# Convolution taps moved to TensorE in 32x32 tiles, in chunks of 32 steps, inside a gated recurrence; state-space scan in slots of four batches

## The chip, the core and the metric

The kernel runs on one NeuronCore of a Trainium2 chip. It uses five engines: TensorE (PE in the rows, PEld for its weight loads), VectorE (DVE), ScalarE (ACT), GpSimd (POOL) and SyncE (SP), which here only issues DMAs. Each engine works through its own list of instructions in the order in which the program wrote them; between engines there are semaphores.

The metric is the device time of the core in microseconds. The kernel before took 2267.38, 2271.31 and 2275.32 us in three runs, 2271.31 in the median.

## The reference, cut to what matters

The input x is [32, 128, 128] (batch, step, feature), the condition [32, 128]. Eight layers follow each other. The first two are those that the change touches: a gated recurrence whose state has 128 features, and a state-space block on what it gives.

```python
def _L0_cond_ref(video, seq, W_z, U_z, C_z, b_z, W_r, U_r, C_r, b_r, W, U, C, b):
    vz = video @ C_z + b_z          # vr, vh alike
    xz = jnp.einsum('btd,de->bte', seq, W_z)     # xr, xh alike
    def step(h, xs):                # 128 steps, one after the other
        z = jax.nn.sigmoid(xzt + h @ U_z + vz)
        r = jax.nn.sigmoid(xrt + h @ U_r + vr)
        hh = jnp.tanh(xht + r * h @ U + vh)
        h_new = (1.0 - z) * h + z * hh

def _mamba2(x, W_in, conv_w, conv_b, dt_bias, A_log, D, init_states, norm_w, W_out):
    # D_INNER 256 = 8 heads x 32, N_STATE 64, CONV_DIM 384, D_CONV 16
    zxbcdt = x @ W_in               # z 256, xBC 384, dt 8
    dt = jax.nn.softplus(zxbcdt[..., -NHEADS:] + dt_bias)
    xBC = silu(causal depthwise convolution of xBC, 16 taps, + conv_b)
    xs, Bm, Cm = xBC[..., :256] (8 heads x 32), xBC[..., 256:320], xBC[..., 320:384]
    dA = jnp.exp(dt * A)            # A = -exp(A_log)
    def step(h, inp):               # h0 = init_states
        h = h * dA_t[:, :, None, None] + einsum('bh,bhp,bn->bhpn', dt_t, x_t, B_t)
        y_t = jnp.einsum('bhpn,bn->bhp', h, C_t)
    y = ys + D[None, None, :, None] * xs
    y = y * jax.nn.silu(z)
    y = y * jax.lax.rsqrt(jnp.mean(y * y, axis=-1, keepdims=True) + 1e-05) * norm_w
    return y @ W_out

def _L0_attn_ref(x, ...):
    y = _mamba2(x, ...)
    t = y / jnp.sqrt(1.0 + y * y)
    return t @ W_nl + b_nl + x
```

Then come a local attention with 16 heads (cond2 in the code), a mixture of experts, an LSTM, an attention with relative positions, a second LSTM and a second mixture of experts. The code of these stages is not changed, but for where the first of them (cprep) puts two transposed weights.

## The kernel before

Everything is kept with features on the 128 partitions. X [128, 32 batches, 128 steps] is the residual, G the output of the running layer. TensorE writes into eight banks of [128, 512] float32, which all carry the name B in the rows; mm (L85), act (L103), stt (L107) and ts (L112) are one-line helpers, so nearly all rows carry their lines, and a group is told by its tiles. The tiles work, catt and spare are large areas in which the stages lay their own buffers.

**Order.** There is no scheduler. For each engine and stage a generator issues instructions and yields; weave (L64) goes round the generators and takes one piece (a turn) of each. The lists of the engines thus come from the number of yields in each generator, written by hand; weave takes a lane out when it has ended.

**Recurrence** (gru_pe L407, gru_act L463, gru_dve L482, gru_pool L509), 22 to 250 us. A step is: the recurrent products of r and z with the tile gzh (mmh, L95: four column strips of 32 for each, since 32 batches are the columns), tanh on ScalarE into gth, VectorE's grh and gq, the product of the candidate with grh, tanh into ghh, VectorE's new gzh. Part of the next step's gate sum is put into the banks ahead with gq. The input products of the block of eight steps ahead (gru_inputs_pe L394, tile X) stand between the gate product and the candidate's, one piece a step, and gru_warm_pe (L448, tile identb) fills TensorE's idle time with a product of 384 columns behind each step and three more every fourth step, whose results are not used. Semaphores make POOL write each state to G.

**State space.** The 32 batches are worked on in eight units of four. Per unit the convolution (conv_pe L668, conv_act L695, conv_dve L736) takes three parts of 128 channels: a projection of G with win, an eviction by ScalarE into a padded buffer XP, taps 0 to 5 on TensorE as products with diagonal matrices (NT = 6, tile tap, 128x512 each), an eviction with the bias cb, and taps 6 to 15 on VectorE, one stt over [128, 512] each with the column cw; then tanh on ScalarE and one product for the SiLU on VectorE. The last part holds B and C in its two halves of 64 partitions.

The scan is done in matrix form, batch by batch, by two lanes (wk 0 and 1; mamba_pe L787, mamba_act L892, mamba_dve L978), which take the units in turn. One batch n of a lane goes: decay (eight scaled copies of the triangle tri, into E, catt in the rows), sums with the matrix low (two products of 512 columns), exponentials, cross (C times B, 64 rows deep, and the transposes of x), cbm and the product E times cbm (L1012), the state product with h0T, thirty-two 32x32 products of the triangle (with E and xdt), the product D x through the diagonal dg, the gate, and y on VectorE (L1020 to L1024). After four batches come norm, W_out, the long reciprocal (L1040), W_nl and two additions to X, the second on POOL (L1054). A unit of four batches has some 26 turns in each lane's list. mdt_pe, mdt_act, mdt_dve (L614 to L640) compute dt and the decays for all batches first.

**Around them.** mprep_load (L554) issues the loads of this stage's small weights on SP's queue; mprep_pe, mprep_act and mprep_dve prepare them inside the recurrence, h0T near its end. cprep, the preparation of the next stage, follows in lane 0's list, and mamba_first_end (L1104) is what it waits for.

## Time and profile before

| | before |
|---|---|
| runs | 2267.38, 2271.31, 2275.32 us |
| profiled execution: its own time / span | 2269.55 / 2267.7 us |
| mean granted TensorE clock | 0.951 |
| PE busy | 2011.8 us (89%), 25711 instructions |
| VectorE busy | 1698.1 us (75%), 3792 |
| ScalarE busy | 1008.1 us (44%), 2835 |
| GpSimd busy | 459.9 us (20%), 794 |

The profiled execution is one of its own. Its time lies 1.8 us under the median of the runs; its span goes from the first to the last instruction. The profile gives the shares of busy time over the whole span, so they mix stages with different limits. A row in order of time joins consecutive instructions of the same kind, and its second number then reaches from the first's start to the last's end.

By landmarks: the recurrence's last gzh starts at 250.0 us, the first decay at 278.9, the convolution's last taps end near 629, the last addition to X starts at 697.1, and the next stage begins at about 700.

### The profile page before, as it was taken

Reading aid. Unit: us, or ns where it says so; the run is one execution under the profiler, and the core shown is the slowest. Engines: PE = TensorE matmul, PEld = TensorE weight load, DVE = VectorE, ACT = ScalarE, POOL = GpSimd, SP = SyncE. Lnnn points to the kernel's source line nnn. Section 1 sums busy time; section 2 is a strip of 40 time slices with the busy share of each in tenths; the row PEclk is TensorE's granted clock in tenths of the full one; section 3 lists DMA queues with packets and bytes.
Section 4 is the critical chain, followed back from the end, with each engine's and each line's share of the span. In section 5 each row is a group of like instructions: output and inputs, shape, how many; then the busy total and the mean of one; then the engine's idle time right before and its main releaser. Section 6 shows DMA issues by size and latency. Waiting matters only on the chain.

```text
span 2267.7 us, 62486 instructions
## 1 busy us (share of the span) xinstructions
PE 2011.8 (89%) x25711; PEld 1278.0 (56%) x25787; DVE 1698.1 (75%) x3792; ACT 1008.1 (44%) x2835; POOL 459.9 (20%) x794
## 2 busy tenths in 40 slices
PE   7888888998886898898799999985999789999998
PEld 5555534444453444343576677763666556677776
DVE  3443489999965888777888888844999668888887
ACT  2333245666553221221555555542544445555555
POOL 2211000000000434336012222243432111121200
PEclk8999699999978999999999999996999999999999
DMA  2000000000010000000311111106553211111111
GB/s 61 3 4 4 2 1 1 1 1 1 1 38 15 0 1 1 1 1 1 112 48 44 44 44 44 39 4 130 107 108 73 65 40 44 39 44 44 44 57 38
DMA packets 76038, 76.61 MB, mean 34 GB/s; under 512 B 15756, under 2 KB 57060, under 8 KB 74180
## 3 DMA queue, kind: packets, MB, share of 16 engines
q1 hardware_dynamic: 71848, 70.11, 12.3%
q8 instruction: 203, 3.33, 0.6%
q10 hardware_dynamic: 3904, 2.49, 0.4%
q14 instruction: 83, 0.68, 0.1%
HBM read 60.09 MB, written 11.82 MB: 32 GB/s over the span
## 4 chain that ended last, share of the span: by engine, by line
PE 47%; DVE 30%; ACT 9%; issue 8%; DMA 1%; POOL 1%; ACTq 1%; SPq 1%; another core or an unknown queue 1%; DVEq 0%; POOLq 0%
PE B L85 46%; DVE work L107 6%; DVE work L2117 4%; DVE hr L2081 3%; DVE work L2125 3%; ACT work L103 2%; ACT hr L103 2%; ACT ltc L103 2%; DVE work L1496 1%; ACT catt L103 1%; DVE gzh L107 1%; ACT ghh L103 1%; DVE work L1040 1%; ACTq L2404 1%; DVE grh L107 1%
## 5 line engine op out<-in xcount | busy, mean ns | idle before, releaser
L85 PE MATMUL B<-gr,wres 128*128 128x512 f32 x1248 | 354.5, 412 | 16.4 <-DVE work L2125 10.1
L103 ACT ACTIVATE work<-B 128x512 f32<-128x512 f32 (+7 forms) x468 | 240.1, 529 | 145.4 <-PE B L85 90.2
L2167 POOL COPY G<-lh 128x32 f32<-128x32 f32 x256 | 148.2, 579 | 680.0 <-DVE lh L107 680.0
L85 PE MATMUL B<-work 128*128 128x128 bf16 (+3 forms) x1408 | 260.3, 312 | 28.0 <-ACT work L103 7.0
L85 PEld LDWEIGHTS B<-gr,wres 128*128 128x128 f32 x1248 | 215.1, 189 | 83.7 <-DVE work L2125 27.4
L103 ACT ACTIVATE hr<-work 128x512 fp32r<-128x512 f32 x272 | 173.0, 636 | 147.0 <-DVE work L2125 77.5
L85 PEld LDWEIGHTS B<-work 128*128 128x128 bf16 (+2 forms) x1408 | 141.4, 127 | 139.1 <-issue 79.9
L2081 DVE TENSOR_TENSOR hr<-work,hr 128x512 fp32r<-128x512 f32 x272 | 186.5, 686 | 8.1 <-ACT hr L103 6.6
L2117 DVE TENSOR_TENSOR work<-work 128x512 f32<-128x512 f32 x256 | 178.9, 699 | 16.1 <-ACT work L103 8.9
L107 DVE SCALAR_TENSOR_TENSOR work<-work,cw 128x512 f32<-128x512 f32 x240 | 179.2, 747 | 5.9
L85 PE MATMUL B<-hr,wres 128*128 128x512 f32 x624 | 178.0, 394 | 1.0 <-DVE hr L2081 1.0
L103 ACT ACTIVATE lth<-B 128x96 f32<-128x96 f32 (+1 forms) x512 | 86.8, 222 | 187.2 <-PE B L85 187.1
L85 PEld LDWEIGHTS B<-lh,lw 128*32 128x32 f32 x8128 | 88.8, 112 | 112.5 <-issue 58.6
L85 PE MATMUL B<-lh,lw 128*32 128x32 f32 x8128 | 117.0, 199 | 24.5 <-DVE lh L107 23.2
L107 DVE SCALAR_TENSOR_TENSOR work<-B,ckc,work 128x512 f32<-128x512 f32 x160 | 116.7, 742 | 27.1 <-ACT work L103 17.7
L103 ACT ACTIVATE catt<-catt 128x512 f32<-128x512 f32 (+3 forms) x141 | 81.8, 594 | 119.6 <-DVE catt L2417 89.4
L85 PEld LDWEIGHTS B<-hr,wres 128*128 128x128 f32 x624 | 117.2, 188 | 28.2 <-DVE hr L2081 1.9
L1496 DVE TENSOR_TENSOR work<-B,work 128x512 f32<-128x512 f32 x160 | 106.7, 681 | 32.2 <-remote 31.6
L107 DVE SCALAR_TENSOR_TENSOR lh<-lth,ltc 128x32 f32<-128x32 f32 x256 | 49.4, 193 | 106.6 <-ACT ltc L103 106.6
L1533 POOL TENSOR_TENSOR work<-work 128x512 f32<-128x512 f32 x64 | 82.2, 1284 | 209.7 <-DVE work L1496 115.5
L85 PE MATMUL B<-gr,hr 128*128 128x512 f32 x384 | 114.1, 434 | 10.0 <-DVE gr L1435 7.0
L85 PE MATMUL B<-X,lw 128*128 128x128 f32 x512 | 122.0, 323 | 0.0
(262 smaller groups left out, 3777.8 us busy)
## 6 DMA issues: line engine op xcount, KB each, us to landing
work<-wdr SPq DMA_DIRECT2D x128, 256.0 KB, 3.1
scr<-catt SPq DMA_DIRECT2D x144, 64.0 KB, 2.8
work<-scr SPq DMA_DIRECT2D x16, 384.0 KB
work<-scr SPq DMA_DIRECT2D x16, 192.0 KB
catt<-in_L_ffn_ew SPq DMA_DIRECT2D x24, 128.0 KB, 2.2
work<-scr SPq DMA_DIRECT2D x16, 128.0 KB
out<-work SPq DMA_DIRECT2D x32, 64.0 KB, 2.2
work<-in_x ACTq DMA_DIRECT2D x2, 512.0 KB, 5.3
```

The source lines that it names most:

```text
L85: return e.matmul(out, lhsT, rhs, start=start, stop=stop, skip_group_check=True)
L103: return e.activation(out, in_, func, bias=bias, scale=scale)
L107: return e.scalar_tensor_tensor(out=out, in0=a, scalar=s, in1=b, op0=op0, op1=op1)
L1040: e.reciprocal(m["tm"][:], m["tm"][:]).then_inc(*inc(me, "tr", i))
L1496: e.tensor_tensor(four(pr[n % 6]), four(B[:]), KP[:, c, :, j:j + 128], ALU.mult).then_inc(*inc(dve, "v", i, c, j))
L1533: e.tensor_tensor(av, u0, u1, ALU.add).then_inc(*inc(f"cd{wk}.pool", i, c))
L2081: e.tensor_tensor(hr[1][:], self.hh[j % 4], hr[0][:].bitcast(F32), ALU.subtract).then_inc(*self.inc("m.dve", "h", li, j))
L2117: e.tensor_tensor(src, self.sg[i], self.Wb[n % 4], ALU.mult).then_inc(*inc("m.dve", "pu", li, k))
L2125: h = stt(e, self.hh[m], U, 0.5, src, ALU.mult, ALU.mult) if li else e.tensor_tensor(self.hh[m], U, src, ALU.mult)
L2167: e.tensor_copy(self.G[:, :, t], self.lh[:, t % 4, :]).then_inc(*inc("l.pool", "h", li, t))
L2404: e.dma_start(self.aQ[u % 4][48 + q:49 + q, :, :], self.anT[16 * q:16 * q + 16, :]).then_inc(*self.dma("at.max", u))
```

## The change

The taps of the convolution leave VectorE altogether. The 384 channels are cut into twelve blocks of 32, and each of the sixteen taps is one call of conv_taps_pe: sixteen products on 32x32 tiles of the array. Tile (i, j) takes rows 32i to 32i+31 (channels) and columns 32j to 32j+31, and its moving operand is 8 batches x 32 steps, so block i of a part goes to bank 4+i and strip j holds the batches 8j to 8j+7. The stationary operand is a diagonal of 32, from the table tap [128, 48, 32] that POOL fills in steps 27 to 29 of the recurrence from id32 and cw.

The convolution goes by chunks of 32 steps instead of by units of batches: 4 chunks x 3 parts = 12 pieces (n), each with 16 tap calls, 4 projections of 8 batches (conv_input_pe, a 256-column product into bank 3 and an eviction by ScalarE) and 4 evictions with bias (in the last four pieces two of them by VectorE). Once the steps of a chunk are known, its convolution can run, so conv_pe and conv_act are called twice in each step of the recurrence from step 32 on, once between the gate and the candidate's product and once behind the step's input products; what is left (conv_rest_pe, conv_rest_act) runs after the recurrence and before both lanes. Up to step 31 warm-up products stand there, fewer than before.

To free banks for it, the recurrence keeps its sums in banks 0 to 2 (gru_place), and the input products of the block ahead move from between the two products to behind the step (gru_ahead_pe, five steps of eight). The conv's output cv is laid out [slot of 4 batches, block, step]: a slot o holds the batches o, o+8, o+16 and o+24, one in each 32 partitions.

The scan takes those slots. The transposes of x are done for half a slot at once (turn, bank 6+wk) and turned on VectorE into xdt and xD (with D in a row drow instead of through the diagonal dg, added in y as one more operation); B and C lie in 32 rows each, so cross and the state product become two products of 32 rows. SiLU (tanh and one product) goes into the lanes, four batches wide. Lane 1 starts 14 turns behind lane 0; a slot has 26 turns, and MAMBA_DT_TURNS and MAMBA_UNIT_TURNS go. The initial state h0T is turned for all four strips (mprep_pe, from step 4 on instead of near the end), the bias cb comes in 48 pieces of 32 rows, D in one load of a row.

```diff
-NT = 6
+CONV_STEP = 32
+CHUNK = 32
-MAMBA_DT_TURNS = 6
-MAMBA_UNIT_TURNS = ((8, 1, 1, 1), (22, 1, 1, 1))
+MAMBA_LAG = 14
@@ tensor (scalar alike; vector weaves mdt_dve with conv_dve first)
         weave(self.gru_pe(e), self.mprep_pe(e))
-        weave((self.mdt_pe(e), 2), chain(self.mamba_pe(e, 0), self.cprep_pe(e)), self.mamba_pe(e, 1), self.conv_pe(e))
+        self.conv_rest_pe(e)
+        weave(chain(self.mamba_pe(e, 0), self.cprep_pe(e)), self.mamba_pe(e, 1))
@@ gru_pe, each step
-            if t % 8 == 0 and t + 8 < T:
-                ahead = chain(self.gru_inputs_pe(e, g + 1, 0), self.gru_inputs_pe(e, g + 1, 1))
-            next(ahead, None)
-            if t % 4 == 0:
-                self.gru_warm_pe(e, t, 3)
+            elif t >= CONV_STEP:
+                next(conv, None)
+            elif t % 2:
+                self.gru_warm_pe(e, t, 1)
             e.wait_ge(*at("gru.rh", t))
...
-            self.gru_warm_pe(e, t, 1)
+            self.gru_ahead_pe(e, t)
+            if t >= CONV_STEP:
+                next(conv, None)
+            else:
+                self.gru_warm_pe(e, t, 1)
@@ gru_ahead_pe
+        g, x = t // 8 + 1, t % 8
+        if g == T // 8 or x > 4:
+            return
...
+        if x < 4:
+            self.gru_inputs_pe(e, g, odd, x // 2)
+        else:
+            self.gru_inputs_z_pe(e, g)
@@ mprep_load
+        for k in range(12):
             for j in range(4):
-                pairs.append((self.dcol[32 * j:32 * j + 32, c:c + 1],
-                              bc(I["L0_attn_D"][4 * c + j:4 * c + j + 1], 0, 32)))
-        for c in range(3):
-            pairs.append((self.cb[:, c:c + 1], col(I["L0_attn_conv_b"][c * 128:c * 128 + 128])))
+                pairs.append((self.cb[32 * j:32 * j + 32, k:k + 1], col(I["L0_attn_conv_b"][32 * k:32 * k + 32])))
@@ mprep_pe
-        for _ in range(T - 6):
+        for _ in range(4):
             yield
         e.wait_ge(*self.at("ld.mamba"))
@@ conv_rest_pe (was mdt_pe)
         for b in range(NB):
             last = mm(e, P[:, b, :], self.G[:, b, :], self.win[:, 640:648], True, True)
         last.then_inc(*self.inc("mdt.pe", "x"))
-        for _ in range(12):
-            yield
+        for _ in self.conv_rest:
+            pass
@@ conv_taps_pe
+        for j in range(4):
+            for i in range(4):
+                r = slice(32 * i, 32 * i + 32)
+                last = mm(e, self.bank[4 + i][32 * j:32 * j + 32, 0:256], self.tap[r, 16 * c + k, :],
+                          self.XP[c][r, 8 * j:8 * j + 8, k:k + CHUNK], k == 0, k == 15)
@@ conv_pe
+        for j in range(4):
+            self.conv_input_pe(e, 0, j)
+            yield
+            yield
+        for n in range(12):
+            k = 0
+            for x in range(20):
+                if x in (12, 14, 16, 18):
+                    if n == 11:
+                        continue
+                    self.conv_input_pe(e, n + 1, (x - 12) // 2)
+                else:
+                    self.conv_taps_pe(e, n, k)
+                    k += 1
+                yield
+            for _ in range(4):
+                yield
@@ conv_out_dve
+        return (2, 3) if n >= 8 else ()
@@ conv_dve: the taps 6 to 15 go
-                for k in range(NT, 16):
...
-                    stt(e, acc, X[:, :, 1 + k:129 + k], self.cw[:, c, k:k + 1], acc, ALU.mult, ALU.add).then_inc(
@@ mamba_pe: cross and the state product
-            mm(e, B2[:, 256:384], cv[0:64, 2, t_], C0[0:64, t_], True, True)
-            for c in range(2):
-                last = e.transpose(B2[:, c * 128:c * 128 + 128], cv[:, c, t_], self.ident[:])
+            for x in range(2):
+                last = mm(e, B2[:, 256:384], cv[r, 8 + x, :], cv[r, 10 + x, :], x == 0, x == 1)
...
-                for c in range(2):
-                    mm(e, B0[:, c * 128:c * 128 + 128], cv[:, c, t_], self.dg[:, c, :], c == 0, False)
-                mm(e, B0[:, 256:512], C0[0:64, t_], self.h0T[:], False, False)
+                for x in range(2):
+                    mm(e, B0[:, 256:512], cv[r, 10 + x, :], self.h0T[r, x, :], x == 0, False)
@@ mamba_dve, per half slot (turned)
+            e.tensor_tensor(m["xdt"][:, hs], B3, bc(self.dth[:, o:NB:8, hs].rearrange("p j h -> p h j"), 3, 32), ALU.mult)
+            e.tensor_tensor(m["xD"][:, hs].rearrange("p h j q -> p h (j q)"), B3.rearrange("p h j q -> p h (j q)"),
+                            bc(self.drow[:, hs], 2, 128), ALU.mult).then_inc(*inc(me, "xd", i, h))
```

What this makes of the lists is seen at three places. First TensorE's list at step 40 of the recurrence; gzh feeds the gate product, grh the candidate's, gq the part put in ahead, X,gw are the input products, identb the warm-up. Before:

```order
L85 MATMUL B<-gzh,gw 32x32 x8
L85 MATMUL B<-X,gw 128x32x4
L85 MATMUL B<-grh,gw 32x32 x4
L85 MATMUL B<-gq,gn 32x32 x8
L85 MATMUL B<-identb 128x384
L85 MATMUL B<-gzh,gw 32x32 x8
```

And now, where "work 32x256 x16" is one call of taps:

```order
L85 MATMUL B<-gzh,gw 32x32 x8
L85 MATMUL B<-work 32x256 x16
L85 MATMUL B<-grh,gw 32x32 x4
L85 MATMUL B<-gq,gn 32x32 x8
L85 MATMUL B<-X,gw 128x32x4
L85 MATMUL B<-work 32x256 x16
L85 MATMUL B<-gzh,gw 32x32 x8
```

The input product has moved from between the gate and the candidate's product to behind the step, and a call of taps stands in both places.

Second, TensorE's list in steps 4 and 5, with what now stands there:

```order
L85 MATMUL B<-gzh,gw 32x32 x8
L85 MATMUL B<-grh,gw 32x32 x4
L85 MATMUL B<-gq,gn 32x32 x8
L85 MATMUL B<-gV,ident 128x256
L85 MATMUL B<-X,gw 128x32x4x2
L85 MATMUL B<-identb 128x384
L85 MATMUL B<-ident,h 32x128 x4
L85 MATMUL B<-gzh,gw 32x32 x8
```

The products "ident,h" turn the initial state; they wait for all loads of mprep_load, and the next step's gate product stands behind them. Before they stood near the step 122.

Third, TensorE's list in the scan, at the end of a unit of one lane beside a batch of the other. Before:

```order
L85 MATMUL B<-work,wout 128x512 x2
L85 MATMUL B<-work 128x512 x3
L85 MATMUL B<-catt,low 128x512 x2
L85 MATMUL B<-work 128x512 x3
L85 MATMUL B<-dg,work 128x128 x2
L85 MATMUL B<-h0T,work 128x256
L85 MATMUL B<-work,catt 32x32 x32
L85 MATMUL B<-G,win 128x512
L85 MATMUL B<-win,G 128x256
L85 MATMUL B<-work 128x128
L817 MATMUL B<-ident,work 128x128 x2
L85 MATMUL B<-work,wnl 128x512
```

And now:

```order
L85 MATMUL B<-work,wout 128x512 x2
L85 MATMUL B<-catt,low 128x512 x2
L85 MATMUL B<-h0T,work 128x256 x2
L85 MATMUL B<-spare,catt 32x32 x32
L85 MATMUL B<-win,G 128x256
L85 MATMUL B<-work 128x128 x2
L85 MATMUL B<-work,wnl 128x512
```

The taps (work 128x512), the projection (G,win) and the diagonal (dg) are gone from between the lane's products; the transposes (L817) have become half a slot at once and stand at the end of a unit.

On VectorE, in the same stretch, before:

```order
L1024 TENSOR_TENSOR work<-work,catt 128x256
L107 SCALAR_TENSOR_TENSOR work<-work,cw 128x512 x3
L1004 TENSOR_TENSOR work<-B,triq 128x128
L1007 TENSOR_TENSOR work<-B,catt 128x256
L1012 TENSOR_TENSOR catt<-catt,work 128x1024
```

And now, at the same operations of a lane (L1102 is cbm, L1105 the product of 1024, L1117 to L1121 are y):

```order
L107 SCALAR_TENSOR_TENSOR catt<-catt,B 128x256
L1102 TENSOR_TENSOR spare<-B,triq 128x128
L1105 TENSOR_TENSOR catt<-catt,spare 128x1024
L107 SCALAR_TENSOR_TENSOR X<-B,bnl,X 128x4x128
L107 SCALAR_TENSOR_TENSOR work<-catt,work 128x512
```

The taps are gone, the products of xdt (L1007) too; a SiLU product of 512 elements stands in some turns.

## Rows read from the trace of the kernel before

**Rows 1.** Busy by stretches: us; PE, PEld, DVE, ACT, POOL (count); clock; DMA; GB/s
```profile
22.00:250.00 228.00, 197.58 (x5532) 122.09 (x5531) 94.73 (x534) 75.57 (x442) 48.50 (x149) 0.95 0.02 4
250.00:262.00 12.00, 11.20 (x53) 11.01 (x52) 0.38 (x2) 0.02 (x1) 0.55 (x4) 0.50 0.00 1
350.00:600.00 250.00, 226.59 (x2044) 116.34 (x2043) 232.59 (x379) 153.33 (x370) 8.86 (x5) 0.99 0.00 1
625.00:650.00 25.00, 20.32 (x178) 10.96 (x179) 18.39 (x38) 15.87 (x38) 1.27 (x1) 0.73 0.01 2
```

**Rows 2.** Groups by shape, 350 to 600 us: busy us, mean ns | idle before
```profile
L107 DVE SCALAR_TENSOR_TENSOR work<-work,cw 128x512 f32<-128x512 f32 x160 | 119.3, 746 | 3.7
L1012 DVE TENSOR_TENSOR catt<-catt,work 128x1024 f32<-128x1024 f32 x22 | 26.7, 1214 | 0.0
L107 DVE SCALAR_TENSOR_TENSOR work<-work 64x512 f32<-64x512 f32 x10 | 11.7, 1166 | 0.3
L85 PE MATMUL B<-work 128*128 128x512 f32 x189 | 85.9, 595 | 2.3 <-ACT work L103 2.3
L85 PE MATMUL B<-G,win 128*128 128x512 f32 x32 | 17.2, 620 | 0.0
L103 ACT ACTIVATE work<-B,cb 128x512 f32<-128x512 f32 x16 | 10.9, 682 | 2.8 <-PE B L85 2.8
L103 ACT ACTIVATE work<-B 128x512 f32<-128x512 f32 x31 | 18.3, 596 | 20.8 <-PE B L875 17.1 <-PE B L85 3.7
```

**Rows 3.** Order of time, one recurrence step: start us, us, engine, instruction
```profile
101.36 0.33 PE L85 MATMUL B<-gzh,gw 128*32 128x32 f32 x16
101.62 0.49 PE L85 MATMUL B<-X,gw 128*128 128x128 f32 x2
102.24 0.27 PE L85 MATMUL B<-grh,gw 128*32 128x32 f32 x8
102.34 0.33 PE L85 MATMUL B<-gq,gn 128*32 128x32 f32 x16
102.61 0.34 PE L85 MATMUL B<-identb 128*128 128x384 bf16 x1
103.06 0.33 PE L85 MATMUL B<-gzh,gw 128*32 128x32 f32 x16
```

**Rows 4.** Tile gzh: ns min/median/max, first and last start us
```profile
L107 DVE SCALAR_TENSOR_TENSOR gzh<-gth,ghh x128: 179/193/771, 27.6 to 250.0; 128x32 f32<-128x32 f32 x128
L85 PE MATMUL B<-gzh,gw x2048: 196/196/263, 22.7 to 248.7; 128*32 128x32 f32 x187
```

**Rows 5.** Order of time, TensorE, on the full array and in three column strips
```profile
569.91 5.33 PE L85 MATMUL B<-work 128*128 128x512 f32 x12
807.45 1.06 PE L85 MATMUL B<-work,selh 128*32 128x512 f32 x6
```

**Rows 6.** SyncE's queue in order of time; DMA issues, us to landing last
```profile
17.69 1.37 SPq L572 DMA_DIRECT2D cb<-in_L_attn_conv_b  x3
cb<-in_L_attn_conv_b SPq DMA_DIRECT2D x3, 0.5 KB, 2.0
```

**Rows 7.** Order of time, TensorE, 250 to 266 us
```profile
250.99 13.82 PE L85 MATMUL B<-win,G 128*128 128x8 f32 x64 [0.80 <-POOL G L112]
```

**Rows 8.** Order of time, state space, from 630 us to its end
```profile
633.04 2.43 ACT L103 ACTIVATE catt<-tri,catt 128x128 f32<-128x128 f32 x8
636.75 3.65 PE L85 MATMUL B<-catt,low 128*128 128x512 f32 x4
646.04 2.43 ACT L103 ACTIVATE catt<-tri,catt 128x128 f32<-128x128 f32 x8
648.52 1.98 PE L85 MATMUL B<-catt,low 128*128 128x512 f32 x4 [0.34 <-ACT catt L103]
655.45 2.44 ACT L103 ACTIVATE catt<-tri,catt 128x128 f32<-128x128 f32 x8
697.11 1.26 POOL L1054 TENSOR_TENSOR X<-X,G 128x512 f32<-128x512 f32 x1 [36.38 <-DVE X L107]
```

509 lines of the change are left out of this document (284 added, 225 removed).

## The prediction, made before the result was known

> **What bounds the kernel now.** On the page PE is the busiest engine, but its share is an average over stages, so the busy time by stretches comes first. In the recurrence (22 to 250 us) no engine is full of useful work: it is a chain of 128 steps. In the state space VectorE is busy 232.6 of 250 us and TensorE 226.6, ScalarE only 153.3 [rows 1]. The reader is to see that both leading engines are full there, and in the second view (groups by shape, 350 to 600 us) with what: on VectorE 160 taps of 746 ns, 119.3 us, and on TensorE 85.9 us of taps and 17.2 us of the convolution's input projection [rows 2]. Last the order of time in three places: a step of the recurrence, tiles side by side in the array, and the end of the state space, where no tap is left.
>
> A step: the gate product starts at 101.36, the candidate's at 102.24, the next gate product at 103.06: 1.70 us, paced by hops PE, ACT, DVE, PE [rows 3]. PE has two holes. The first runs from +0.26 (another tile shape enters 0.26 us after the sixteen gate records begin) to +0.88, the second from +1.25 to +1.70. The 127 intervals from 27.6 to 250.0 us [rows 4] are 1.75 us in the mean.
>
> **The change, part by part.** Sums are against the profiled execution, 2269.55 us (span 2267.7); the runs' median, 2271.31, is 1.8 higher.
>
> *1. Price of a tap call:* 16 matmuls on 32x32 tiles, 256 columns, a pair of records each (every f32 matmul shows as two). On the full array twelve records of 512 columns take 5.33 us, 0.44 each, so 0.22 for 256 columns. Three column strips take 1.06 us for their six records of 512 [rows 5]: strips run at once, a strip's two halves behind each other. If all sixteen tiles do, a call lasts 1.06 - 0.44 (256 columns) + 13 more tiles x 8 ns (sixteen gate records end within 0.33 us [rows 3] where one lasts 0.20 [rows 4]) = 0.72 us by the record. The next shape can start 0.06 us before such an end, as the warm-up does behind the sixteen records of 102.34 (102.61 against 102.34 + 0.33 [rows 3]): 0.66 net. Back to back I take 0.46. No row shows tiles that differ in their 32 rows, so 0.66 is one end; the others are the rivals B (1.30) and E (3.7). I take 0.66, since the row with tiles shows overlap.
>
> *2. A load ahead of step 4.* The convolution's bias comes in 48 pieces instead of 3, D in one instead of 8: 38 more issues of SP at 1.37/3 = 0.46 us, 18 us. Today the last is issued at 19.06 us and lands 2.0 us later [rows 6]; now at about 39. PE used to wait for these loads only near the end of the recurrence; now the turned copies of the initial state stand in step 4, some 7 us after 27.6, at 34.8. The whole chain stands behind them: 4 us, plus 1 for the clock, whose mean of 0.95 in this stage [rows 1] says that it falls at times. +5.
>
> *3. Recurrence, steps 32 to 127.* 192 holes take 126 tap calls and 30 input projections. First hole, 48 taps: 0.26 + 0.66 = 0.92 against 0.88, +0.04, 2 us. An input (0.49 us for two records of 128 columns [rows 3], + 0.22) costs about as much as it has slack. Second hole, 78 taps: 1.25 + 0.66 = 1.91 against 1.69, +0.22. But the next block's input products now stand there too, ahead of the tap, in five steps of eight: 0.49 us by the record, 0.43 net [rows 3], the fifth with twice the columns, +0.22. That gives 0.22 / 0.65 / 0.87 in 3 / 4 / 1 of 8 steps, 0.52 in the mean; 70 x 0.52 + 8 x 0.22 (no block ahead after step 119) = 38. Sum +40 us. ACT is busy 75.6 of 228 us in this stage [rows 1], so I take it that its evictions of 256 columns (under the 0.60 of 512 [rows 2]) fit its gaps. POOL's three products for the tap table stand in steps 27 to 29, covered by the two steps of slack that VectorE leaves it.
>
> *4. The rest of the convolution* cannot hide: both lanes start behind it. 32 small products take 13.8 us today [rows 7], mostly at the lower level (granted 0.50 [rows 1]), so some 7 at the upper one; I take 8. Then 66 tap calls x 0.46 = 30, 14 inputs x 0.72 = 10, and five stalls for evictions, one of 1.9 us (ACT alone) and four of 0.9: 5.5. Together 54 us: from 295 (250 + 40 + 5) to 349 us. VectorE's softplus chain lies beside it.
>
> *5. State space.* The floor of what stays, per unit (one batch; 22 in those 250 us, by the L1012 row): ACT 153.3 less the convolution's 30 (10.9 + 32 x 0.60) over 22 is 5.6, plus 0.5 for the tanh: 6.1 us. TensorE 226.6 - 103.1 over 22: 5.6. It loses the diagonal product and gets two 32-row matmuls in place of each 64-row one, not shown: from nothing to twice their time, and neither is on the way to more than the ACT figure. VectorE 232.6 less 119.3, 11.7 and some 7 (SiLU) [rows 2] over 22 is 4.3; plus some 1.2 for the SiLU and the two 128x512 products of a half slot: 5.5. Hence 32 x 6.1 = 195 us at least.
>
> But a lane is a chain: decay (2.43), sums (1.98), state and tile products, gate product, tanh, next decay. From 646.04 to 655.45, without taps and with the other lane in its norm, a unit takes 9.4 us; from 633.04 to 646.04, in part at the lower clock (the sums took 3.65) and with the last SiLU, 13.0 [rows 8]. A lane spends ten of a slot's 26 turns outside its units, and the lanes are 14 turns apart. So of a slot pair's eight units four run beside the other's norm, two at 9.4 and two at 10.5 (the 13.0 at the upper level, without SiLU): 40 us. The other four share ten turns, bound by ACT at 5.6 each: 22 us. With 4 us for spells at the lower level 66 us, 2.54 a turn; now it is 8 x 250/22 = 91 us. Lane 1 ends after 124 turns: 28 alone at 9.4/4 = 2.35, 66 us, and 96 x 2.54 = 244. Sum 310, from 349 to 659 us.
>
> The last addition to X starts at 697.1 us now [rows 8]. 659 against 697: -38 us. Later stages keep their instructions. 2269.6 - 38 = 2232.
>
> **Rivals.**
> A, the forecast: 2232.
> B, slower: *row tiles of one column strip wait for each other*. A tile's second half, standing ahead of the next row tile in its strip, holds it back: five spans of 0.22 instead of two, +0.64 a call; it decides above 0.86 us a call. Every hole is already overfull: 126 x 0.64 = 81, and 66 x 0.64 = 42 behind: 2355. For it: strips visibly keep their own order; against it: nothing but that strips are independent.
> C, *the scan goes at the lower clock level*. The dense taps leave it; today, where they end, the granted clock is 0.73 [rows 1]. With the tail's units at 13.0 a turn takes 3.05: 96 x 3.05 + 28 x 2.7 = 368, +58, less 3: 2287, slower too. Against it: at 648.52 the sums are back at 1.98 [rows 8].
> D, *the lanes pack to the engines' floor*: 52 us per pair, 96 x 2.0 + 28 x 2.1 = 251, -59: 2173. For it: VectorE is 93% busy today.
> E, *strict order*: half, half, next tile, one after the other: 17 x 0.22 = 3.7 us a call, 192 x 3.0 = 580 more, some 2800. Against it: in strict order the three strips would need four times 0.44, not 1.06 in all [rows 5].
> E is what the Trainium skill states ("TensorE: Matmul & The Clock Gate", Part 3: matmuls start and end in program order); the rows for column strips disagree with it. The same part measures 10.6 times for sixteen tiles, which speaks for A; no row here shows row tiles.
>
> **How the numbers follow.** A 0.43, D 0.18, B 0.24, C 0.14, E 0.01. 0.3% (6.8 us) is what a measurement can tell from no change. A's own spread (+-30 us) puts 0.37 of it under the bound, 0.04 inside, 0.02 over; D is all faster; C has 0.02 faster and 0.02 the same. Faster 0.57, same 0.06, slower 0.37. The range goes from a little under D to B: 2168 to 2357; A's own is 2202 to 2262.
>
> **What would show it.** Right: recurrence steps of 1.75 to 2.4 us after step 32; tap calls of 0.7 us with sixteen tiles overlapping; a stall of 4 us at step 4; the last step near 295, the first decay near 349; a slot pair in 66 us. B: calls over 1.2 us, steps over 2.6. C: a granted clock under 0.8 from 350 to 660 us, sums of 3.6 us. D: ACT over 90% busy. Wrong altogether if later stages move by over 5 us.

## The result, and the profile after

The changed kernel takes 2379.99 us in the median of four runs (2373.37 to 2391.22), the kernel before 2271.23 us in four: ratio 1.0484, 95% interval 1.0436 to 1.0532. It is slower by some 109 us, where 2232 was forecast and the range ended at 2357. The profiled execution took 2384.33 us, its span 2382.1.

| stretch, us | before | forecast | after | after less forecast |
|---|---|---|---|---|
| first gzh to step 32 | 60.0 | 65 | 82.2 | +17 |
| steps 32 to 127 | 162.5 | 202 | 248.3 | +46 |
| last step to first decay | 28.8 | 54 | 90.8 | +37 |
| first decay to last addition to X | 418.2 | 310 | 353.7 | +44 |
| from there to the end | 1570.6 | 1571 | 1581.0 | +10 |

A stretch is read from the starts of gzh's products on VectorE, of the first decay and of POOL's last addition. The last row is no effect of the change: in the runs below, whose instructions there are the same, it lies anywhere from 1569 to 1582. The other four are where the forecast failed. They vary too from trace to trace where the lists are the same: steps 32 to 127 take 242.6 to 251.9 us in nine traces with the lists of the changed kernel, the scan 349.4 to 355.8 in ten; the first stretch repeats within 1 us. A smaller difference between two traces shows nothing.

The busy time by stretches of the changed kernel, with the columns of [rows 1] and to be held against them:

```profile
22.00:107.00 85.00, 68.07 (x1436) 41.49 (x1435) 25.79 (x135) 19.70 (x111) 20.99 (x57) 0.58 0.04 3
107.00:357.00 250.00, 219.79 (x8018) 119.76 (x8017) 65.79 (x382) 75.59 (x380) 33.16 (x101) 0.93 0.02 4
357.00:447.00 90.00, 74.83 (x2207) 49.30 (x2206) 15.23 (x37) 10.95 (x29) 2.16 (x4) 0.85 0.01 3
447.00:801.00 354.00, 274.98 (x2760) 150.92 (x2760) 203.33 (x369) 210.39 (x517) 10.97 (x9) 0.76 0.02 7
```

The reader is to see two things. In the scan no engine is full any more (TensorE 78%, ScalarE 59%, VectorE 57%), so the floors of the engines, from which half of the forecast's part 5 (state space) is worked out, bound nothing. And the granted clock is 0.58 in the early recurrence and 0.76 in the scan.

The first four lines of what TensorE waited for, 22 to 447 us (us in total, times, longest):

```profile
PE B L85 <- issue: 23.2, 36, 1.2
PE B L85 <- DVE grh L107: 18.8, 32, 1.4
PE B L85 <- DVE work L112: 7.8, 3, 3.0
PE B L85 <- DMA cb<-in_L_attn_conv_b: 4.6, 1, 4.6
```

The fourth line is the load of part 2 of the forecast: 4.6 us for 4 forecast. The second is the first hole of a step, where no input product stands any more: 18 of its 32 waits, 11.2 us, lie before step 32, where the kernel before has two of 1.1 us together. The first line is one that the forecast does not have, and it is the largest: "issue" is a wait for nothing that the profile shows. In order of time, TensorE with its records in two steps of the recurrence (start us, us, engine):

```profile
...
187.27 0.65 PE L85 MATMUL B<-work 32*32 32x256 f32 x11 [0.95 <-issue]
187.84 0.27 PE L85 MATMUL B<-grh,gw 128*32 128x32 f32 x8
187.93 0.31 PE L85 MATMUL B<-gq,gn 128*32 128x32 f32 x16
188.17 0.77 PE L85 MATMUL B<-work 32*32 32x256 f32 x32
188.87 0.33 PE L85 MATMUL B<-gzh,gw 128*32 128x32 f32 x16
189.13 0.76 PE L85 MATMUL B<-work 32*32 32x256 f32 x32
189.82 0.27 PE L85 MATMUL B<-grh,gw 128*32 128x32 f32 x8
189.90 0.23 PE L85 MATMUL B<-gq,gn 128*32 128x32 f32 x5
191.00 0.32 PE L85 MATMUL B<-gq,gn 128*32 128x32 f32 x11 [0.86 <-issue]
```

A call of taps (32 records) takes 0.76 us, near the forecast's 0.72, but TensorE stops in the middle of one call (21 of its records stand before the first row), and again in the middle of sixteen gq records, whose operand has been there since the first five. The first time it idles 0.95 us, the second 0.86. Behind the recurrence, where calls follow each other:

```profile
434.73 2.75 PE L85 MATMUL B<-work 32*32 32x256 f32 x128
438.20 2.76 PE L85 MATMUL B<-work 32*32 32x256 f32 x128 [0.72 <-issue]
441.67 2.76 PE L85 MATMUL B<-work 32*32 32x256 f32 x128 [0.71 <-issue]
```

After every 128 records it stands still for 0.71 us. 128 records with their 128 weight loads are 256 entries, and the transfers of the instruction queue are 16 KB each. In 40 us of the recurrence, 180 to 220 us, there are eight of them before and eleven after:

```profile
q8 instruction: 8, 0.13, 1.4%
```

```profile
q8 instruction: 11, 0.18, 2.2%
```

So 256 entries would be one such transfer (64 bytes each, worked out and not shown by a row). The changed kernel makes one per 3.6 us where the one before made one per 5, and back to back it gets one per 3.47 us. The times of the transfers fit: from 428 to 447 us there are four, which start at 432.38, 435.89, 439.33 and 442.81 us, and TensorE goes on 2.3 us behind each, at 434.73, 438.20, 441.67 and 445.14. I take it that this is the pace at which TensorE is supplied here; the experiments test it.

### The profile page after: what moved, and what is told of

It is laid out like the page before. It is cut to its first block, busy times and chain, and to the rows that moved or that the text cites. A ratio compares the mean times of both kernels' runs of the same rounds, so it can differ in the third digit from the quotient of the medians.

```text
span 2382.1 us, 73929 instructions
## 1 busy us (share of the span) xinstructions
PE 2078.9 (87%) x31509; PEld 1311.7 (55%) x31509; DVE 1544.3 (65%) x3565; ACT 1010.8 (42%) x2862; POOL 467.0 (20%) x806
## 4 chain that ended last, share of the span: by engine, by line
PE 56%; DVE 22%; ACT 9%; issue 8%; SPq 2%; DMA 1%; ACTq 1%; POOL 1%; DVEq 0%; POOLq 0%
PE B L85 54%; DVE work L2220 4%; DVE work L107 3%; DVE hr L2184 3%; DVE work L2228 3%; ACT catt L103 2%; ACT hr L103 2%; ACT ltc L103 2%; SPq L630 1%; ACT work L103 1%; ACTq L2507 1%; DVE work L1599 1%; DVE lth L107 1%; DVE lpq L107 1%; DVE gr L2034 1%
## 5 line engine op out<-in xcount | busy, mean ns | idle before, releaser
L85 PE MATMUL B<-work 32*32 32x256 f32 (+2 forms) x7328 | 294.0, 385 | 27.1 <-issue 11.2
L103 ACT ACTIVATE work<-B 128x512 f32<-128x512 f32 (+6 forms) x480 | 236.8, 509 | 174.0 <-PE B L85 131.7
L85 PEld LDWEIGHTS B<-work 32*32 32x32 f32 (+2 forms) x7328 | 162.6, 108 | 124.4 <-issue 75.8
L85 PE MATMUL B<-lh,lw 128*32 128x32 f32 x8128 | 116.9, 199 | 24.5 <-DVE lh L107 23.2
L85 PE MATMUL B<-catt,low 128*128 128x512 f32 x128 | 96.2, 898 | 38.8 <-ACT catt L103 33.4
L107 DVE SCALAR_TENSOR_TENSOR grh<-gth,gh 128x32 f32<-128x32 f32 x128 | 28.0, 218 | 143.4 <-ACT gth L103 143.4
```

What stands on the lines that cost most here:

```text
L85: return e.matmul(out, lhsT, rhs, start=start, stop=stop, skip_group_check=True)
L103: return e.activation(out, in_, func, bias=bias, scale=scale)
L107: return e.scalar_tensor_tensor(out=out, in0=a, scalar=s, in1=b, op0=op0, op1=op1)
```

## Experiments

Positions are those of the profiled execution; the totals are medians of four runs, the ratios are to the kernel before, timed beside it.

### a1, a2: the wait for the load, and the warm-up

a1, of the changed kernel (its other half delays ScalarE's copy likewise):

```diff
 def mprep_pe
-        for _ in range(4):
+        for _ in range(20):
             yield
```

> The turned copies of the initial state move from steps 4 to 7 of the recurrence to steps 20 to 23, behind the landing of the bias pieces; nothing else changes. Theory 'the wait lets the clock fall': in the changed kernel TensorE waits 4.6 us in step 4, the granted clock falls to 0.50 at 38 us and comes back only at 120 us, and steps 5 to 35 cost some 2.5 us instead of 1.9. Without the wait the clock stays up: the recurrence ends some 20 us earlier (336 instead of 356.6), total near 2360. Rival 'only the wait': 5 us, total near 2375, and the clock falls all the same, because the warm-up has become thin.

a2 adds the old amount of warm-up below step 32:

```diff
-            elif t % 2:
-                self.gru_warm_pe(e, t, 1)
+            elif t % 4 == 0:
+                self.gru_warm_pe(e, t, 3)
```

> As a1, and up to step 31 the warm-up of the kernel before (three products more every fourth step, in place of one in every odd step). If the clock falls for the thin warm-up and not for the wait, a1 gains 5 us and this one 20; if the wait was the cause, both end alike within 3 us; if the clock falls in both, the low level belongs to something else that the change put there (the input products behind the step).

Measured: a1 2371.58 us (ratio 1.0451, 1.0434 to 1.0469), a2 2370.03 us (1.0449, 1.0417 to 1.0482); step 32 starts at 100.2 and 103.7 us instead of 108.4. The stop of 4.6 us is gone, and the stretch up to step 32 is 9.0 us shorter in a1 (73.2 for 82.2), 4.7 in a2. So the theory that the wait alone lets the clock fall is wrong (20 us expected); "only the wait" (5 us, and the clock falls all the same) is nearer, and the old warm-up does not bring the clock back: from 38 to 90 us it is 0.64 and 0.60 (0.50 in the changed kernel, 0.90 before). The trace of a2 shows what the forecast had not priced. First the kernel before at the lower level, then a2 at the same level:

```profile
47.53 0.44 PE L85 MATMUL B<-gzh,gw 128*32 128x32 f32 x16
47.90 0.80 PE L85 MATMUL B<-X,gw 128*128 128x128 f32 x2
48.63 0.34 PE L85 MATMUL B<-grh,gw 128*32 128x32 f32 x8
48.76 0.42 PE L85 MATMUL B<-gq,gn 128*32 128x32 f32 x16
49.11 0.50 PE L85 MATMUL B<-identb 128*128 128x384 bf16 x1
49.54 0.44 PE L85 MATMUL B<-gzh,gw 128*32 128x32 f32 x16
```

```profile
46.05 0.44 PE L85 MATMUL B<-gzh,gw 128*32 128x32 f32 x16
47.00 0.33 PE L85 MATMUL B<-grh,gw 128*32 128x32 f32 x8 [0.51 <-DVE grh L107]
47.18 0.44 PE L85 MATMUL B<-gq,gn 128*32 128x32 f32 x16
47.55 0.80 PE L85 MATMUL B<-X,gw 128*128 128x128 f32 x2
48.14 0.52 PE L85 MATMUL B<-identb 128*128 128x384 bf16 x1
48.59 0.44 PE L85 MATMUL B<-gzh,gw 128*32 128x32 f32 x16
```

Before, the input product X fills the first hole and a step at the lower level takes 2.01 us without a gap. Now the hole stands empty (0.51 us idle) and X stands in the step's own path: 2.54 us. It costs once in the step, and TensorE idles in addition; whether that keeps its level low is what c2 asks.

### b1, c2: the input products back in the first hole, and filling

b1 is a1 with the input products of r and the candidate between the gate and the candidate's product again, two steps later (z's share a bank with what ScalarE reads there, so they stay); c2 is b1 with more warm-up up to step 31: one or three products in the first hole and two behind each step. The edit of b1:

```diff
+                if t >= 2 and (t - 2) % 8 < 4:
+                    self.gru_ahead_pe(e, t - 2)
...
-            self.gru_ahead_pe(e, t)
+            if t % 8 == 4:
+                self.gru_ahead_pe(e, t)
```

> As a1, and the input products of r and the candidate for the block ahead go back between the gate product and the candidate's, two steps later than now (steps 2 to 5 of a block; z's stays behind step 4 because of its bank). Theory 'the empty hole and the input products in the path': up to step 31 a step loses the 0.8 us of input products at the lower level and TensorE no longer idles 0.5 us in the first hole, so the clock comes back by 60 us as in the kernel before: the recurrence ends 15 to 20 us earlier than in a1 (348), with step 32 starting at 88 to 92 instead of 100. Rival 'something else holds the clock down' (taps, chip): step 32 within 3 us of 100. From step 32 on both agree on no gain: one hole loses what the other gets.

> As b1, with warm-up products in the first hole and two behind every step up to step 31. If the low clock in steps 5 to 31 comes from thin filling together with the moved input products, step 32 now starts at 85 to 90 us as in the kernel before (96.6 in b1, 100.2 in a1, 108.4 in the changed kernel), and the total is 5 to 10 us under b1's; if it starts at 96 again, the filling is not it.

Measured: b1 2365.11 us (1.0413, 1.0383 to 1.0442), step 32 at 96.6, the recurrence ends at 344.4; c2 2355.22 us (1.0365, 1.0334 to 1.0397), step 32 at 90.3, its end at 332.3. In c2 the granted clock is 1.00 from 38 to 90 us. b1 alone gave less than half of what was expected, 3.6 us where it was 8 to 12 at step 32; with the filling, step 32 is back within 3 us of the kernel before (87.6). The first miss is thereby taken apart. Of the 22.2 us by which the stretch from the first gzh to step 32 grew (60.0 to 82.2), taking away the wait for the load gives back 9.0 (a1: 73.2), the input products back in the hole 3.2 (b1: 70.0) and the filling 6.1 (c2: 63.9); 3.9 stay open. So the load is the largest part, twice the 4.6 us of its stop. The shares are for this order of edits.

### a3: all taps behind the recurrence

```diff
-CONV_STEP = 32
+CONV_STEP = 128
```

> All 192 calls of taps and all 48 projections behind the recurrence, warm-ups in their place. Theory 'the holes are worth it': the recurrence ends near 260 to 270 us (86 us of the steps from 32 on and part of the low clock go), then 192 calls of 0.87 us (0.69 and a quarter of a 0.7 us stop), 48 projections of 0.7 and twelve waits of 2.7 us: 230 us, first decay near 505 us instead of 447, total near 2435. Rival 'the holes are as dear as the place behind': first decay within 15 us of 447 and a total within 15 us of 2380, because each call in a hole lengthens its step by almost what it costs behind.

Measured: 2482.93 us (1.0945, 1.0919 to 1.0970), the recurrence ends at 318.1 us, the first decay starts at 548.7: 101 us later than in the changed kernel, nearly twice the 58 that were expected. The recurrence then runs at the lower level for 244 of its 291 us (102 of 330 in the changed kernel, 20 of 222 before) and ends at 318 instead of 260 to 270. The part behind takes 230.6 us, as worked out (230). The holes are worth using: the rival, no difference, is wrong by 100 us.

### a4, d1, b2, c4: what a call of taps is bound by

a4 puts four products of 96 columns on the full array in place of the sixteen, d1 (on top of c2) eight on 64x64 tiles, b2 keeps table and input in bfloat16, c4 swaps the two loops.

```diff
 a4, conv_taps_pe
+        if 0 < k < 15:
+            for i in range(4):
+                mm(e, self.bank[4 + i][:, 0:96], self.ident[:], self.XP[c][:, 8 * i:8 * i + 8, k:k + 12], False, False)
+            return
 d1, conv_taps_pe
+                        mm(e, self.bank[4 + 2 * i + h][64 * j:64 * j + 64, 0:256], self.ident[r, 64 * i:64 * i + 64],
+                           self.XP[c][r, 8 * j:8 * j + 8, k:k + CHUNK], False, False)
 b2, lay_mamba
-        self.tap = ar(128, 48, 32)
-        self.XP = [ar(128, NB, CHUNK + 15) for _ in range(3)]
+        self.tap = ar(128, 48, 32, dt=BF16)
+        self.XP = [ar(128, NB, CHUNK + 15, dt=BF16) for _ in range(3)]
 c4, conv_taps_pe
-        for j in range(4):
-            for i in range(4):
+        for i in range(4):
+            for j in range(4):
```

> In place of the sixteen 32x32 products of calls 1 to 14 of every block of taps, four products on the full array of 96 columns each (the taps' values are left out, calls 0 and 15 stay): 8 records of some 85 ns, 0.68 us of array time as before, with a quarter of the instructions. Theory 'TensorE is starved of instructions': its stops that nothing releases (30 times, 19 us up to 360 us, and eight of 0.53 to 0.82 us behind) go, the recurrence ends 20 us earlier and the rest behind it is 10 us shorter: total near 2350. Rival 'the holes are too short for 0.7 us': the stops go elsewhere or cost nothing, total 2372 to 2385.

> The table of taps and the padded input are kept as bfloat16, so each of a call's sixteen products shows as one record instead of two: half the instructions of a call and a quarter of the columns' time (the taps are less exact by this). In the changed kernel calls that follow each other take 0.69 us and TensorE then stops 0.7 us after every 128 records. Theory 'a call is bound by the instructions': back to back a call takes half, 0.33 to 0.36 us, the stops that nothing releases halve (36 times to under 20), the recurrence ends near 315 and the first decay near 380; total near 2310. Rival 'bound by the columns' (16 tiles' 256 columns pass one after another per strip): 0.2 us a call or less. Rival 'the holes are not the cause': recurrence still over 345.

> The sixteen tiles of a call go in the other order: the column strip changes from product to product instead of the rows. In the changed kernel a call's 32 records take 0.71 to 0.76 us, 0.69 when calls follow each other. If a call is bound by the rate at which products start, nothing changes: a call in 0.69 to 0.76 us, total within 8 us of 2380. If tiles of one strip hold each other back, a call is shorter (0.5 us) and the total falls by over 15 us; if tiles of the same rows do, it gets longer.

> As c2, but calls 1 to 14 of every block of taps go on 64x64 tiles: eight products of 256 columns instead of sixteen (the taps' values are left out, since the identity stands in place of the table). Each tile still passes two products one after the other, 0.43 us by the columns' time, with half the instructions. Theory 'stops for instructions': back to back a call takes 0.45 us, hardly any stop in the recurrence is left, a step from 32 on costs 2.1 to 2.2 us instead of 2.55 (242 us for 95 steps in c2), so the recurrence ends near 295 instead of 332, and the part behind it takes 65 instead of 88: total near 2295. Rival 'hole too short, instructions do not matter': recurrence within 8 us of c2's.

Measured: a4 2440.26 us (1.0744, 1.0706 to 1.0782), b2 2342.5 us (1.0288, 1.0249 to 1.0327), c4 2382.53 us (1.0494, 1.0474 to 1.0513), d1 2360.13 us (1.0384, 1.0367 to 1.0400, against 1.0365 of c2).

a4's stops are gone up to its first decay (none is left), as the theory of the instructions has it, but its time got worse: the clock is at the lower level for 256 of 395 us of the recurrence, which its expectation did not have; why is not shown. So a4 does not price the stops, hence d1. c4: nothing changes, so neither strips nor rows hold a call back. b2, TensorE behind the recurrence:

```profile
388.21 1.90 PE L85 MATMUL B<-work 32*32 32x256 bf16 x117 [1.87 <-DVE work L112]
391.62 2.00 PE L85 MATMUL B<-work 32*32 32x256 bf16 x128 [1.51 <-issue]
395.36 0.43 PE L85 MATMUL B<-work 32*32 32x256 bf16 x11 [1.75 <-issue]
```

Up to its first decay b2 stops 8 times for "issue", 8.4 us, where the changed kernel stops 36 times, 23.2 us. Its recurrence is 27 us shorter (303.1) although 239 us of it are at the lower level. (b2's profiled execution, 2325.66 us, was the fastest of its four runs, 17 under their median.)

d1's own price was wrong: a call on 64x64 tiles takes 1.03 us, not 0.45 (from the start of the first line to that of the second), so that the recurrence ended at 337.4 and not near 295. That is within 8 us of c2's 332.3, the very bound of the rival "instructions do not matter"; the total alone cannot tell the two apart:

```profile
203.69 1.09 PE L85 MATMUL B<-work,ident 64*64 64x256 f32 x16
204.71 0.27 PE L85 MATMUL B<-grh,gw 128*32 128x32 f32 x8
```

The waits can. What TensorE waited for from step 32 to the end of the recurrence, c2 and then d1:

```profile
PE B L85 <- issue: 18.7, 27, 1.7
PE B L85 <- DVE gzh L107: 6.7, 18, 0.4
PE B L85 <- DVE grh L107: 4.4, 8, 0.6
```

```profile
PE B L85 <- DVE gzh L107: 6.4, 18, 0.4
PE B L85 <- DVE grh L107: 4.4, 8, 0.6
```

All stops are gone and the other waits are the same. d1's calls are 0.34 to 0.38 us longer (1.03 against 0.65 to 0.69 net, from a call's start to the next tile's), 14 of 16 of the 126: 37 to 42 us more; its steps 32 to 127 took 247.6 us where c2's took 242.0, 6 more. So the stops cost an estimated 31 to 36 us there, give or take the 5 us by which this stretch varies, and more than the 18.7 that show as idle. The difference lies in slow calls, as that of 1.40 us instead of 0.71 at 202.31 us in the changed kernel; that they are slow for the same reason is not shown by itself.

### b3, c1, d2, e2: level and table loads in the scan

b3 puts two unused products before the sums of three batches in four, c1 ten there and four before the state product; d2 replaces the norms' square roots by copies, e2 is c1 with d2.

```diff
 c1, mamba_pe
                 yield
+                if j:
+                    self.fill_pe(e, B3, 10)
                 if n < 15:
                     sums(n + 1)
                 yield
                 if j:
+                    self.fill_pe(e, B3, 4)
 d2, mamba_act (the same for m["tm"])
-            act(e, m["ss"][:], m["ss"][:], ACT.Sqrt).then_inc(*inc(me, "sr", i))
+            act(e, m["ss"][:], m["ss"][:], ACT.Copy).then_inc(*inc(me, "sr", i))
```

> In the scan two unused products of 384 columns stand before the sums of three batches in four, where TensorE waits for the decays. Theory 'the scan goes at the lower level': granted 0.76 over 354 us in the changed kernel (172 us at the lower level, the sums 1061 ns in the median instead of 592); with the holes filled the clock rises over 0.9 and the scan takes 325 us or less: total near 2350. Rival 'the chain of a lane is paced by ScalarE and VectorE': the clock rises but the scan stays within 8 us of 354. Third way: the products delay the other lane's sums by 0.7 us each, 24 times a lane, and the scan gets longer, 365 or more.

> Two such products in b3 were too few: 384 columns in bfloat16 are 0.16 us at the upper level, TensorE was still idle a fifth of the scan, the lower level went from 172 to 135 us and the scan from 353.7 to 352.1. Here, in the changed kernel, ten stand before the sums of three batches in four (where TensorE waits 2.2 us for the decays) and four before the state product. Theory 'the lower level stretches the lanes' chains' (sums 3.7 us instead of 2.0, once or twice a unit): lower level under 80 us, scan 325 us or less, total near 2350. Rival 'the lanes are held by ScalarE's order (table loads and the norm's square root between a batch's decay and its exponentials)': the scan stays within 8 us of 354 even at the upper level. If the products themselves delay the other lane: over 362.

> In the changed kernel, the square roots of the norms are replaced by copies (those values are left out), so ScalarE no longer loads a table before and behind each: up to 32 loads of 1.28 us in the scan. Theory 'ScalarE's order holds the lanes' (at 630.3 to 633.1 and 644.4 to 647.6 us one lane's loads stand between the other's sums and its exponentials): 16 pairs of loads, 41 us of ScalarE, of which more than half is on a lane's chain: scan 325 to 335 instead of 353.7, total near 2360. Rival 'something else, the loads lie beside waits': scan within 8 us of 354.

> c1 and d2 in one: the scan filled as in c1, and the norms' square roots replaced by copies (those values are left out), so no table loads. If the two waits hide each other, the scan gains far more than 5 + 3 us: 325 to 335 instead of 353.7. If they do not, it takes 344 to 347, the sum of the two, and the lanes are held by the order of the lists and the chain itself.

| kernel | total us | ratio, interval | at the lower level | scan us |
|---|---|---|---|---|
| changed | 2379.99 | 1.0484, 1.0436 to 1.0532 | 172 | 353.7 |
| b3 | 2373.46 | 1.0440, 1.0417 to 1.0463 | 135 | 352.1 |
| c1 | 2373.66 | 1.0456, 1.0434 to 1.0478 | 83 | 349.0 |
| d2 | 2381.02 | 1.0475, 1.0459 to 1.0490 | 172 | 350.9 |
| e2 | 2367.16 | 1.0418, 1.0397 to 1.0439 | 61 | 341.6 |

Ten traces whose scan lists are those of the changed kernel take 349.4 to 355.8 us, so b3, c1 (4.7 us) and d2 (2.8 us) by themselves show no clear gain; each time the rival ("within 8 us of 354") was right. Both together give 12.1 us, which is clear, in the scan as in the total. It is more than the sum of 7.5 that was expected if the two do not hide each other, and far from 325 to 335. How they can hide each other is seen in the changed kernel's scan:

```profile
640.50 0.60 ACT L103 ACTIVATE spare<-B 128x512 f32<-128x512 f32 x1 [2.50 <-PE B L85]
640.99 2.43 ACT L103 ACTIVATE catt<-tri,catt 128x128 f32<-128x128 f32 x8
643.47 3.78 PE L85 MATMUL B<-catt,low 128*128 128x512 f32 x4 [3.01 <-ACT catt L103]
644.35 1.28 ACT L103 ACT_TABLE_LOAD   x1
646.30 1.28 ACT L103 ACT_TABLE_LOAD   x1
647.59 1.08 ACT L103 ACTIVATE catt<-B 128x512 f32<-128x512 f32 x2
```

Lane 0's decays (640.99) stand behind a square of lane 1 for which ScalarE waits 2.50 us. Then come the sums, at the lower level until 647.2, and ScalarE's loads around lane 1's square root until 647.58, so that the exponentials (647.59) are late by either. In c1 the same place reads:

```profile
642.25 1.98 PE L85 MATMUL B<-catt,low 128*128 128x512 f32 x4 [1.39 <-ACT catt L103]
643.13 1.28 ACT L103 ACT_TABLE_LOAD   x1
645.07 1.28 ACT L103 ACT_TABLE_LOAD   x1
646.37 1.08 ACT L103 ACTIVATE catt<-B 128x512 f32<-128x512 f32 x2
```

The sums now end at 644.23, 2.1 us before ScalarE is free, and the exponentials start 4.12 us behind the sums' start in both kernels: here the level's gain is swallowed whole by the loads. The filling may also delay the other lane elsewhere; no run separates that, so c1 does not bound what the level costs.

### d3, e1: the offset of the lanes

```diff
-MAMBA_LAG = 14
+MAMBA_LAG = 16
```

> In the changed kernel lane 1 starts 16 turns behind lane 0 instead of 14. If the lanes are held by what stands in front of them in an engine's list (as ScalarE's square behind W_out, which waits 2.5 us for TensorE with the other lane's decay behind it), another offset moves every such meeting and the scan changes by 5 to 20 us either way; two turns more for lane 1 alone would be +5. If the floor of the engines bound the lanes, it changes by those 5 only.

> In the changed kernel lane 1 starts 12 turns behind lane 0 instead of 14. d3 (16) made the scan 25.5 us longer where two turns alone are worth 5. If the lanes collide less the nearer they start (both then have their norm further from the other's units' start), the scan takes 330 to 345; if 14 is the best place of the lists, it is longer than 358 on this side too; within 5 us of 349 if only the two turns count.

Measured: 16 turns 2406.77 us (1.0585, 1.0568 to 1.0603), scan 379.2; 12 turns 2397.17 us (1.0558, 1.0531 to 1.0585), scan 368.8; 14 turns 353.7. Two turns are worth 5 us by themselves; they cost 25, and two fewer cost 15. Neither the engines' floors nor the length of the lists gives that, so what stands in front of what in the lists matters, and 14 is the best of the three. The level moved as well (213 us of the scan at the lower one with 16, 184 with 12, 172 with 14), and no run separates the two.

### b4, c3, d4: towards a better version

b4 is a1, b1 and b3 in one. c3 is c2 with b2 and c1, and with two products of zeros (full array, 256 columns) in each call of taps.

> a1, b1 and b3 in one. If the three causes add up: 9 us (a1), 15 to 20 (b1) and 28 (b3), total 2325; if b3's gain is none, 2350.

> All that helped or may help in one: late turned copies, input products in the first hole, taps and padded input in bfloat16, filling in the recurrence (two products of zeros with 256 columns added in each call of taps) and in the scan. b2's recurrence lay at the lower level for 243 of 303 us. If the level is what a step costs there, the recurrence takes 255 to 270 us, the part behind it 65, the scan 325 to 350: total 2250 to 2290, near the kernel before. If the instructions bound the steps even so: recurrence 300 and total near 2320.

Measured: b4 2355.84 us (1.0355, 1.0331 to 1.0378), near the case without a gain from b3; c3 2428.31 us (1.0687, 1.0647 to 1.0728), a miss. Its recurrence ends at 385.9 us, with 218 us of it at the lower level. Full-array products between tiles do not slip in; each takes its turn, and a call grows to 1.3 us, here at the lower level:

```profile
204.54 0.41 PE L85 MATMUL B<-work 32*32 32x256 bf16 x8
204.89 0.39 PE L85 MATMUL B<-work,zb 128*128 128x256 bf16 x1
205.21 0.41 PE L85 MATMUL B<-work 32*32 32x256 bf16 x8
205.55 0.39 PE L85 MATMUL B<-work,zb 128*128 128x256 bf16 x1
```

d4 starts from the kernel before: taps on the full array where they stood, all sixteen, in bfloat16.

```diff
-NT = 6
+NT = 16
-        self.tap = self.area([self.work, 74 * 256 - 3 * NT * 128], [128, 3 * NT, 128])
+        self.tap = self.area([self.spare, 0], [128, 3 * NT, 128], BF16)
-        self.XP = [ar(128, 4, 144) for _ in range(3)]
+        self.XP = [ar(128, 4, 144, dt=BF16) for _ in range(3)]
 conv_dve: no taps left
-                    stt(e, acc, X[:, :, 1 + k:129 + k], self.cw[:, c, k:k + 1], acc, ALU.mult, ALU.add).then_inc(
```

> The kernel before with all sixteen taps on TensorE's full array in bfloat16 (table and padded input in bfloat16, less exact by this), none on VectorE. VectorE loses 240 taps of 0.746 us, 179 us; TensorE gives up 144 products of 0.89 us, 128, and gets 384 of 0.22, 84. Over 350 to 600 us VectorE would go from 232.6 to 113 us and TensorE from 226.6 to some 197; the scan falls from 418 us to 340 to 355 (as the changed kernel's, by the lanes' chains), total near 2200. If the lanes were held by something else than VectorE's taps, it stays over 2250.

Measured: 2229.69 us (2224.72 to 2238.62), ratio 0.9812, interval 0.9785 to 0.9839: 42 us faster than the kernel before and 150 faster than the changed one. It was expected near 2200. Its scan takes 377.8 us, not 340 to 355. From 350 to 600 us, to be held against the third of [rows 1] and the fourth of [rows 2]:

```profile
350.00:600.00 250.00, 223.51 (x2369) 119.89 (x2368) 137.97 (x260) 173.45 (x412) 8.61 (x6) 0.96 0.01 1
```

```profile
L85 PE MATMUL B<-work,spare 128*128 128x512 bf16 x256 | 60.6, 384 | 2.4 <-ACT work L103 2.4
```

VectorE went from 232.6 to 138 us (113 expected), TensorE is nearly as busy as before (223.5 for 226.6) while more units pass in the 250 us. The price is the precision of the taps.

## Why the prediction was wrong, step by step

*Price of a tap call* (0.72 us by the record, 0.66 net): right for a call without a stop, 0.71 to 0.76 in the holes. Rivals B and E fall, c4 confirms it. Wrong is "back to back I take 0.46": it is 0.69 by the array and 0.87 with the stops. The forecast had counted columns and overlap, and nowhere the instructions: 64 entries a call, at a pace of 256 per 3.47 us or more. By the Trainium skill ("TensorE: Matmul & The Clock Gate", Part 3) a set of tiles takes one product's time and some 4 ns for each further tile. With two halves of 0.22 us for the product that would be an estimated 0.50 us a call; the trace has 0.65 to 0.69 net, so the measurement decides; why it is longer is not shown.

*A load ahead of step 4* (+5): the wait was right (4.6 for 4 us), the sum was not. The stretch grew by 22 us. The forecast gave the clock 1 us, and it priced the input products behind the step only from step 32 on. The load cost 9 us in all (a1), the input products' new place 3 (b1), the thinner filling with the lower level 6 (c2: granted clock 1.00 for 0.50 from 38 to 90 us); 4 stay open.

*Steps 32 to 127* (+40): steps without a stop cost what was forecast. A step with two calls takes 1.90 to 1.98 us (1.91 forecast), with an input product 2.39 (2.34). The stops make most of the difference, an estimated 31 to 36 us of the 46 by c2 and d1; the forecast's sum has no term for them. The remaining 10 to 15 stay open: c2, whose level is up from the start, takes 242.0 instead of 248.3, but b3, with the lists of the changed kernel, takes 242.6.

*The rest of the convolution* (54 us, measured 90.8): 66 calls at 0.87 instead of 0.46 are 27 of the 37 us; the small products took 12.1 us, not 8 (4 more); the waits for evictions took 9.7 us, not 5.5 (4 more): three of them are 2.6 us in the mean (7.8 us in the waits above) where 0.9 was taken. 2 us stay open.

*State space* (310 us, measured 353.7): the wrong step is "two at 9.4 and two at 10.5 ... the other four share ten turns". A slot pair takes 79 us, not 66: the lanes hardly share, each lane's four units lie beside the other's norm, and a unit there takes 12 to 17 us in lane 0 (its products with E start at 613, 627, 639 and 656) and 10 to 12 in lane 1. Rival D falls with it: no engine is near its floor. The 5.6 us a unit of those four also leave out the 0.5 us of tanh that the forecast had itself added to ScalarE's floor, 2 us a pair. The 9.4 came from one place near the end of the kernel before, where the other lane was in its norm too, but its square fell into ScalarE's wait for the sums, and its table loads (651.16 and 653.88 us) behind the exponentials. In the changed kernel ScalarE waits 2.50 us for the other lane's W_out with the decays behind it, the sums take 3.78 us, and the loads stand before the exponentials. The 13.0 of the unit before it, which the forecast brought down to 10.5, was nearer to what came. Rival C was right in its mechanism (sums 1061 ns in the median against 592 before, granted 0.76) and its 368 was nearer than 310, but the level alone is worth some 5 us by c1, within the spread, and 9 between d2 and e2. 12 of the 44 us are shown (e2); d3 and e1 show that another offset in the lists moves more than that, and how much of the remaining 32 an ideal order would give stays open.

## What to carry to other kernels

Price small tiles by instructions as well as by columns: in the trace, find the longest back-to-back run of such records and look whether TensorE stops there with "issue"; here it did where 256 records and weight loads were wanted in less than some 3.5 us. When an edit empties one gap of a chain and fills another, what goes into the path and what the idle gap does to the clock must both be counted, from the first step on. And a unit's time read at one place of two interleaved lists belongs to that place: look for what of the other lane stands between its operations there before it is taken as a price.

## What the runs showed of the hardware that was not expected

- Back to back, 128 records with their 128 weight loads (by the estimate above one transfer of 16 KB) pass per 3.47 to 3.75 us in most float32 stretches (4.14 at most, granted clock 1.00) and per 3.74 us in the bfloat16 one (granted clock 0.50), though the records themselves take 2.76 and 2.00 us. So the one stretch at half the clock is no slower than the slower float32 ones.
- Sixteen 32x32 tiles of 256 columns take 0.65 to 0.69 us in float32; eight products on 64x64 tiles take 1.03, longer with half the records.
- The busy share of the profile does not tell the granted clock: from step 32 to the last, TensorE shows as busy 302 of 313 us in a4 and the clock is 0.70; in c2 it is 211 of 242 us and 0.96. Why is not shown.
